# Feed-forward by pairs of batches, with the image attention of batches 2 and 3 in four half-batches inside it

## The reference

```python
x = x + _L0_xattn_ref(ctx_512, _layernorm(x), ...)       # graph attention, two layers
x = x + _L0_ffn_ref(_layernorm(x), ...)                  # 8 experts, two of them per row
x = x + _L1_xattn_ref(_layernorm(x), ctx_512, ...)       # image attention
x = x + _L1_ffn_ref(_layernorm(x), w_gate, w_up, w_down) # feed-forward, 2048 hidden columns

# image attention: p is the normalised x
kv = k_v @ W_k.T + b_k
out = einsum('bij,bjd->bid', p, kv)
sim = einsum('bid,bjd->bij', out, kv) * scale
sim = (sim - mean) * rsqrt(var + EPS) * ln_gamma + ln_beta
attn = softmax(sim)
# feed-forward: of each four hidden columns the two largest are kept
h = silu(x @ w_gate) * (x @ w_up)
out = keep_two_of_four(h) @ w_down
```

## Time and profile before

| | |
|---|---|
| median of 3 runs | 1154.78 us (1154.68 to 1155.99) |
| the profiled execution | 1155.69 us, its span 1154.0 us |
| PE busy | 976.8 us, 85% of the span |
| DVE, ACT, POOL busy | 649.3, 375.2, 264.2 us |
| bytes moved | 85.33 MB, 74 GB/s on the mean |
| mean granted TensorE clock | 0.914 |

### The profile page before, as it was taken

One profiled execution on the slowest core, in us unless ns is written; L12 is line 12 of the kernel. 1 busy time (PEld: TensorE's weight loads), 2 busy tenths in 40 slices (PEclk: granted clock), 3 DMA queues, 4 the chain that ended last, 5 costly groups with the idle time before them and its releaser, 6 DMA issues. The chain is left out here.

```text
span 1154.0 us, 15603 instructions
## 1 busy us (share of the span) xinstructions
PE 976.8 (85%) x4579; PEld 811.2 (70%) x4580; DVE 649.3 (56%) x1383; ACT 375.2 (33%) x640; POOL 264.2 (23%) x296
## 2 busy tenths in 40 slices
PE   4997459999999974333568799999999999999996
PEld 3873259999999962222456688888888888888884
DVE  7986744423443226867887445656445455664444
ACT  5875144323333323234334112222222212222120
POOL 0564033320424104467133002010030101110000
PEclk8998679999999995666679899999999999999998
DMA  8357055422634214412012001110020100000001
GB/s 315 76 139 224 10 199 172 165 99 72 204 122 145 79 40 121 149 41 69 1 37 73 1 1 37 37 35 1 0 73 0 36 0 18 18 1 1 37 37 73
DMA packets 35421, 85.33 MB, mean 74 GB/s; under 512 B 5936, under 2 KB 6064, under 8 KB 34096
## 3 DMA queue, kind: packets, MB, share of 16 engines
q1 hardware_dynamic: 26800, 61.72, 15.4%
q0 software_dynamic: 8576, 23.08, 7.6%
HBM read 61.97 MB, written 22.81 MB: 73 GB/s over the span
## 5 line engine op out<-in xcount | busy, mean ns | idle before, releaser
L72 PE MATMUL ps<-f_x_lo,f_w_hi 128*128 128x512 f32 x512 | 203.0, 396 | 13.5 <-POOL f_w_lo L1398 6.8
L73 PE MATMUL ps<-f_x_hi,f_w_lo 128*128 128x512 f32 x512 | 201.9, 394 | 0.0
L74 PE MATMUL ps<-f_x_hi,f_w_hi 128*128 128x512 f32 x512 | 201.6, 394 | 0.0
L1460 DVE TENSOR_TENSOR f_hid<-moe_rows,ps 128x512 f32<-128x512 f32 x64 | 43.7, 684 | 198.6 <-ACT moe_rows L1455 198.4
L72 PEld LDWEIGHTS ps<-f_x_lo,f_w_hi 128*128 128x128 f32 x512 | 97.7, 191 | 35.3 <-DVE f_hid L1460 7.2
L1455 ACT ACTIVATE moe_rows<-ps 128x512 f32<-128x512 f32 x64 | 38.3, 600 | 229.3 <-PE ps L74 229.1
L74 PEld LDWEIGHTS ps<-f_x_hi,f_w_hi 128*128 128x128 f32 x512 | 97.7, 191 | 20.8
L73 PEld LDWEIGHTS ps<-f_x_hi,f_w_lo 128*128 128x128 f32 x512 | 97.8, 191 | 20.4
L72 PE MATMUL ps<-gu_w_lo,m_xT_hi 128*128 (+1 forms) x312 | 106.1, 340 | 4.0 <-DVE m_xT_lo L1704 3.8
L72 PE MATMUL ps<-f_w_lo,kv_c_hi 128*128 128x512 f32 x256 | 102.3, 400 | 5.4 <-DVE x L2299 5.4
L73 PE MATMUL ps<-f_w_hi,kv_c_lo 128*128 128x512 f32 x256 | 102.2, 399 | 0.0
(11 more groups left out here) (300 smaller groups left out, 1951.3 us busy)
## 6 DMA issues: line engine op xcount, KB each, us to landing
raw<-in_moe_gu SPq DMA_DIRECT2D x32, 352.0 KB, 4.3
y_scratch<-m_y SPq DMA_DIRECT2D x39, 256.0 KB, 2.2
raw<-in_ffn_gu SPq DMA_DIRECT2D x16, 512.0 KB, 3.5
raw<-in_moe_dn SPq DMA_DIRECT2D x24, 256.0 KB
x<-in_x SPq DMA_DIRECT2D x4, 1024.0 KB, 12.0
gat_rows<-g_ybuf SPq DMA_DIRECT2D x16, 256.0 KB, 3.3
xn_scratch<-g_xn SPq DMA_DIRECT2D x16, 256.0 KB, 4.2
raw<-in_ffn_dn SPq DMA_DIRECT2D x16, 256.0 KB, 2.9
```

Of the source, the lines that this page charges most:

```text
L72: eng.matmul(out, lhs_hi, rhs_lo, start=start, stop=False)
L73: eng.matmul(out, lhs_lo, rhs_hi, start=False, stop=False)
L74: return eng.matmul(out, lhs_hi, rhs_hi, start=False, stop=stop)
L1460: dve.tensor_tensor(out, sg[:, k, :], self.UP[k], ALU.mult).then_inc(self.hid_made, 1)
```

## The change

The feed-forward takes the batches in pairs: first the four quarters of batches 0 and 1 (units 0 to 7), then those of 2 and 3 (units 8 to 15), so every weight is loaded and split twice. The image attention's block does only batches 0 and 1, and keeps the keys of batches 2 and 3. Their attention is done inside units 1 to 7 in four halves of 256 rows (h = 0 to 3). A slot is one part of one unit (slot 4n + j stands ahead of part j of unit n + 1), and a half's steps have fixed slots, counted from 6h: -1 and 0 gather the expert rows, 0 and 1 add them, 2 ACT's row sums (two passes over the row), 3 power -1/2 and normalised rows, 4 transposes, 5 `out`, 6 scores and centring, 7 scaling and exponential, 8 the sum into `X` and ACT's row sums for the feed-forward, 9 their power. The operands of batches 2 and 3 are normalised at slots 24, 25, 27, 28 and transposed at 25, 26, 28, 29. PSUM: three banks for gate and up in turn, three for the down sums, two for the attention. Silu waits for gate alone. The loops are written out. In the diff `early` holds ACT's copies (slots 6h + 4 and 6h + 5, and those of the operands), `late` its row sums (6h + 2, 6h + 8), normalised rows (6h + 3) and exponentials (6h + 7).

```diff
@@ class Units
-        self.GATE = [ps[:, 0, :], ps[:, 1, :]]
-        self.UP = [ps[:, 2, :], ps[:, 3, :]]
-        self.ACC = [ps[:, 4 + i, :] for i in range(TB)]
+        self.GU = [ps[:, k, :] for k in range(3)]
+        self.ACC = [ps[:, 3 + k, :] for k in range(3)]
...
+    def act_gate_up(self, act, s, r):
+        uses = RQ // self.SLOTS
+        act.wait_ge(self.ld_gu[r % self.SLOTS], 16 * (uses * s + r // self.SLOTS + 1))
+        if s >= 1:
+            act.wait_ge(self.products, RQ * (PAIR * s - 1) + r + 1)
+        act.copy(self.w_hi[r][:, 0:2, :], self.raw_gu[:, r % self.SLOTS, :, :]).then_inc(self.gate_up_hi, 1)
...
+    def pe_gate_up(self, pe, n, r):
...
+        for j, bank in ((0, self.gate_bank(n, r)), (1, self.up_bank(n, r))):
+            m = 2 * (RQ * n + r) + j - 3
+            if m >= 0:
+                pe.wait_ge((self.silu, self.hid_made)[m % 2], m // 2 + 1)
...
+            ins.then_inc((self.gates, self.products)[j], 1)
...
+    def pe_down(self, pe, n):
...
+        for i in range(TB):
+            if TB * n + i >= 3:
+                pe.wait_ge(self.acc_free, TB * n + i - 2)
...
@@ ffn, SyncE
+                for s in range(1, UNITS // PAIR):
+                    for r in range(2):
+                        u.load_gate_up(sp, dram["ffn_gu"], s, r)
+                    for r in range(RQ):
+                        u.load_down(sp, dram["ffn_dn"], s, r)
+                    for r in range(2, RQ):
+                        u.load_gate_up(sp, dram["ffn_gu"], s, r)
...
@@ ffn, GpSimd
+                for n in range(UNITS - 1):
+                    s, second = divmod(n + 1, PAIR)
+                    for j in range(RQ):
+                        slot_work(RQ * n + j)
+                        if second and s + 1 < UNITS // PAIR:
+                            u.pool_gate_up(pool, s + 1, j)
+                        if second and s >= 1 and j < 2:
+                            for r in (2 * j, 2 * j + 1):
+                                u.pool_down(pool, s, r)
@@ ffn, TensorE
+                for n in range(UNITS):
+                    if n + 1 < UNITS:
+                        for j in range(RQ):
+                            slot_work(RQ * n + j)
+                            if j == 0 and n + 1 in (PAIR * Q, PAIR * Q + 1):
+                                pe.wait_ge(lo_done[1], TB * (n + 2 - PAIR * Q))
+                            u.pe_gate_up(pe, n + 1, j)
+                    u.pe_down(pe, n)
@@ ffn, ScalarE
+                def row_sums(k, t, m):
...
+                    act.activation(junk[:, :], X[:, t, :], ACT.Identity,
+                                   accum_out=total[:, k, m:m + 1]).then_inc(totalled[k], 1)
+                    act.wait_ge(totalled[k], m + 1)
+                    act.activation(nmean[:, k, m:m + 1], total[:, k, m:m + 1], ACT.Identity,
+                                   scale=-1.0 / D).then_inc(meaned[k], 1)
+                    act.wait_ge(meaned[k], m + 1)
+                    act.activation(junk[:, :], X[:, t, :], ACT.Square, bias=nmean[:, k, m:m + 1],
+                                   accum_out=square[:, k, m:m + 1]).then_inc(squared[k], 1)
...
+                for n in range(1, UNITS):
+                    s, second = divmod(n, PAIR)
                     for r in range(RQ):
+                        slot = RQ * (n - 1) + r
+                        early(slot)
+                        u.act_silu(act, n, r, sg)
+                        if second and s + 1 < UNITS // PAIR:
+                            u.act_gate_up(act, s + 1, r)
+                        if second and s >= 1 and r < 2:
+                            for k in (2 * r, 2 * r + 1):
+                                u.act_down(act, s, k)
+                        late(slot)
+                    sparsify(n)
@@ ffn, VectorE
+                for n in range(1, UNITS):
+                    for r in range(RQ):
+                        slot_work(RQ * (n - 1) + r)
+                        if r == 0:
+                            dve.wait_ge(u.hid_lo_done, u.LOS * n)
+                        u.dve_hid(dve, n, r, sg, hid[:, r, :])
+                    keep_two(n, 0)
+                    evac(n - 1, (0, 1))
+                    keep_two(n, 1)
+                    for h in range(2):
+                        split(n, h)
+                    evac(n - 1, (2, 3))
+                evac(UNITS - 1, range(TB))
```

More of the change, by code:

```diff
@@ L1376, in load_down @@
[L1376 to L1388, removed]
@@ L1399, in pool_gate_up, with pool_down @@
                            self.w_hi[r][:, 0:2, :].bitcast(F32), ALU.subtract).then_inc(self.gate_up_lo, 1)
-    def pool_down(self, pool, u, r):
-        pool.wait_ge(self.down_hi, self.R * u + (r + 1))
+    def pool_down(self, pool, s, r):
+        pool.wait_ge(self.down_hi, RQ * s + r + 1)
         pool.tensor_tensor(self.w_lo[r][:, 2, :], self.raw_dn[:, r, :], self.w_hi[r][:, 2, :].bitcast(F32),
                            ALU.subtract).then_inc(self.down_lo, 1)
[L1408 to L1422, removed]
@@ L1437, in pe_rest @@
[L1437 to L1445, removed]
-            self.pe_down(pe, self.U - 1, c)
-    def act_silu(self, act, u, c, r, sg, first=False):
-        act.wait_ge(self.products, self.at(u, c, r) + 1)
-        if not (first and r < 2):
-            act.wait_ge(self.hid_made, self.at(u, c, r) - 1)
-        k = self.bank(c, r)
-        act.activation(sg[:, k, :], self.GATE[k], ACT.Silu).then_inc(self.silu, 1)
@@ new lines, in act_silu, with dve_hid @@
+    def act_silu(self, act, n, r, sg):
+        k = RQ * n + r
+        act.wait_ge(self.gates, k + 1)
+        if k >= 2:
+            act.wait_ge(self.hid_made, k - 1)
+        act.activation(sg[:, k % 2, :], self.gate_bank(n, r), ACT.Silu).then_inc(self.silu, 1)
+    def dve_hid(self, dve, n, r, sg, out):
+        k = RQ * n + r
+        dve.wait_ge(self.silu, k + 1)
+        dve.wait_ge(self.products, k + 1)
+        dve.tensor_tensor(out, sg[:, k % 2, :], self.up_bank(n, r), ALU.mult).then_inc(self.hid_made, 1)
@@ L2135, in ffn, with feed_at, four @@
+        def feed_at(m):
+            c, i = divmod(m, TB)
+            s = slice(P * i, P * i + P)
+            return u.x_hi[c][:, :, s], u.x_lo[c][:, :, s]
+        def four(bank):
+            return bank.rearrange("p (d n) -> p d n", d=DC)
         with nc.Block() as block:
@@ L2167, in _, with turn @@
             def _(pe):
-                turns = iter(range(TB, T))
-                def turn_two():
-                    for t in islice(turns, 2):
-                        norm.pe_turn(pe, t)
-                turn_two()
-                u.pe_gate_up(pe, 0, 0, tiles=range(1, RQ), first=True, between=turn_two)
-                pe.wait_ge(norm.lo_done, T)
-                u.pe_rest(pe)
+                def turn(i, k, m):
+                    pe.wait_ge(xn_ready[k], m + 1)
+                    for d in range(DC):
+                        ins = pe.transpose(AT[i][:, P * d:P * d + P], xn[:, i, P * d:P * d + P], ident[:, :])
+                    ins.then_inc(turned[k], 1)
@@ L2257, in keep_two, with add_rows @@
-                def keep_two(q, c, h):
-                    links = LINKS * 4 * q + LINKS * c + 4 * h
+                link = chain.link
+                def add_rows(h, k):
+                    for i in range(2):
+                        t = PAIR * TB + 2 * h + i
+                        dve.wait_ge(got[i], 16 * (2 * h + k + 1))
+                        if k == 1:
+                            dve.wait_ge(added, 4 * h + i + 1)
+                        dve.scalar_tensor_tensor(out=X[:, t, :], in0=xn[:, i, :], scalar=rt["weight"][:, t, k:k + 1],
+                                                 in1=X[:, t, :], op0=ALU.mult, op1=ALU.add).then_inc(added, 1)
```

687 lines of the change are left out of this document (409 added, 278 removed).

## The result

The changed kernel is slower: median 1174.87 us (1173.97 to 1176.61, four runs) against 1154.73 (1154.26 to 1155.99) in the same session, ratio 1.0167 with an interval of 1.0155 to 1.0180 (the two medians alone give 1.0174, which lies inside it). Its profiled span is 1172.4 us against 1154.0, +18.4; the mean granted clock 0.911.

A forecast was written before the change was run, and what follows sets the result against it. PE bounds the feed-forward units; it is mostly idle in the attention ahead. Terms -57.3 - 6.3 + 18.7 + 43.8 + 11.5 + 6.7 sum to +17.1, 1172 us in the runs, taken as 1170 for overlapping waits; range 1138 to 1190.

The forecast's parts named there:

- The block's start: Feed-forward block's start: two batches of attention leave the front, so it starts at 536 instead of 593.3, -57.3 us (-52 to -61).
- The 27.5 us of DVE's work for batch 1: Before PE's first part: 18 us of batch 1's own work plus 9.5 for statistics, normalising, two transposes' wait and `lo`.
- The first unit: Start of the block to unit 1's gate and up end: 4 tiles turned, not 12, -6.3 us (-3 to -8).
- PE's added work: Attention inside the units: four half-batches of 3.9 us, plus 3.2 for turning 8 tiles, +18.7 us (17 to 22).
- PE's waits in units 1 to 8: PE waiting for down banks, row sums and normalised rows in in-order queues: +43.8 us (19 to 65).
- rival 1: Waits in the units close up because DVE and ACT have room: faster, 1139 us; chance 0.22.
- The clock: Matmuls at the lower clock behind the five waits over 4 us: +11.5 us (0 to 30).
- Units 9 to 15: Fourth down tile waits 2.2 us in units 9, 11, 13, late third load adding nothing beyond: +6.7 us (0 to 10).
- Rival 2: Whole kernel breaks even, with stalls of 45 us in all: 1155 us; chance 0.07.
- Rival 4: On ACT, a Silu/exponential table switch holds it twice the row's 1.28 us, eight times: 1177 us; chance 0.05.
- Rival 3: PE's clock does not recover: units 3 to 8 have ten waits, 2.8 us each, delays handed on: 1194 us; chance 0.10.
- Rival 5: Less than two batches leaves the front; if the feed-forward block starts at 545, 1179 us; chance 0.06.

The follow-up runs named there:

- the best version: Changed kernel plus four edits: first down bank freed earlier, weight loads asked for earlier, row sums two slots later, unit 7's rows ahead of weight copies: 1142.55 us, ratio 0.9882.

## Why the prediction was right, and where its terms were off

The forecast was 1170 us and slower; it came at 1174.87. The direction and the mechanism were right: the front gains two batches of attention, and the in-order queues, the third down bank and the lower clock behind the waits take more than that back. The closeness is in part luck. The sum was +17.1 and the span gave +18.4, but under it the terms were off by up to 8 us in both directions: the start by +4.0, the waits of units 1 to 8 by -8.4, the clock there by +3.0, the units behind by +5.2. Two of the signs that would have shown it wrong were near: under 30 us of waits (35.4 came), and a block that ends after 540 (it ended at 540.0).

*The block's start*: -53.3 instead of -57.3, in the bounds. The step "Batch 0 runs as it did, less POOL's adds beside it: it ends near 501" failed: batch 1's first centring starts at 502.97, before at 502.46. From batch 0's first centring (471.51, before 470.51) that is 31.5 us instead of 32.0, so POOL's adds had held up half a microsecond at most; the other 1.0 was lost ahead of that, and differs between executions: without the attention in the units, with the same front, PE's first part comes 1.2 us earlier (530.03). The 27.5 us of DVE's work for batch 1 held well: PE's first part comes at 531.23, 28.3 later. In it lie 2.88 us of DVE waiting for the third tile's scores, and one scaling of 2.90 us instead of 0.74 beside POOL's first subtraction; the 7.4 for the part itself came as 8.3. The chain (DVE twice, POOL, PE):

```profile
513.35 0.74 DVE L1994 SCALAR_TENSOR_TENSOR kv_c_raw<-kv_c_raw,a_rs,k_beta 128x512 f32<-128x512 f32 x1
...
521.14 2.90 DVE L1994 SCALAR_TENSOR_TENSOR kv_c_raw<-kv_c_raw,a_rs,k_beta 128x512 f32<-128x512 f32 x1
...
521.16 2.33 POOL L1394 TENSOR_TENSOR f_w_lo<-raw,f_w_hi 128x1024 fp32r<-128x1024 f32 x1
...
531.23 0.79 PE L73 MATMUL ps<-f_x_lo,f_w_hi 128*128 128x512 f32 x1 [1.93 <-DVE f_x_lo L169]
```

*The first unit*: -6.8, as predicted (-6.3), with the wait for Silu that was named (5.77 us, to 580.15, 40.2 us behind the block's start; 40.6 predicted).

*PE's added work*: about 17.6 instead of 18.7; twelve matmuls of 256 columns take 1.43 us, 0.119 each, where 0.14 was taken between two sizes.

*PE's waits in units 1 to 8*: 35.4 instead of 43.8; this term was the worst sized. The places were right, nearly every size too large: slot 10 7.39 for 9.6 (its own times, 20.8 less 10.9, give 9.9), slot 26 5.86 for 6.3, slot 25 3.04 for 3.4, slot 22 1.67 for 2.6, unit 7's bank 1.04 for 2.9, unit 4's 2.35 for 5.6. The longest single wait was unit 5's for a bank, not slot 10's as said, though the four in front of transposes still add to more (18.0) than the six for a bank (13.8). Even units without attention had none, as said. A row sum was taken as 1.9 us, and takes 1.84:

```profile
655.75 0.63 ACT L2264 ACTIVATE raw<-x 128x512 bf16<-128x512 f32 x1
...
656.74 0.72 ACT L2270 ACTIVATE raw<-x,f_nmean 128x512 bf16<-128x512 f32 x1
...
663.09 0.58 ACT L1435 ACTIVATE moe_rows<-ps 128x512 f32<-128x512 f32 x1
```

Four tiles hold ACT from 655.75 to the next Silu at 663.09, 7.3 us (7.5 predicted): rival 1's condition, "if a row sum costs under 1 us", is refuted. What made the sum too large is, most likely, that each wait was counted from the undelayed schedule; PE's earlier pauses gave ACT and DVE time for the next. The run that frees the first bank earlier shows this from the other side: with 17.8 us of bank waits gone, the waits for rows, `lo` and products grew by 9.4.

One place was too small: unit 5's bank, 7.79 for 4.3. The prediction had the power behind the subtraction whose weights land late, and that is there. It had neither the gather that DVE waits for in the same slot nor the collision behind both. DVE, then POOL and ACT:

```profile
763.60 1.82 DVE L2362 SCALAR_TENSOR_TENSOR x<-moe_rows,weight,x 128x512 f32<-128x512 f32 x2 [5.49 <-DMA moe_rows<-y_scratch,slot]
765.38 2.90 DVE L2381 SCALAR_TENSOR_TENSOR kv_c_raw<-kv_c_raw,kv_wk_raw,k_beta 128x512 f32<-128x512 f32 x1
...
770.29 0.68 DVE L1441 TENSOR_TENSOR f_hid<-moe_rows,ps 128x512 f32<-128x512 f32 x1
...
761.81 2.40 POOL L1394 TENSOR_TENSOR f_w_lo<-raw,f_w_hi 128x1024 fp32r<-128x1024 f32 x1 [2.21 <-ACT f_w_hi L1384]
764.16 1.18 POOL L2182 TENSOR_TENSOR kv_wk_raw<-kv_wk_raw,minus_half 128x2 f32<-128x2 f32 x1
765.33 2.39 POOL L1394 TENSOR_TENSOR f_w_lo<-raw,f_w_hi 128x1024 fp32r<-128x1024 f32 x1
...
760.68 1.05 ACT L1384 CAST f_w_hi<-raw 128x1024 fp32r<-128x1024 f32 x1 [6.31 <-DMA raw<-in_ffn_gu]
```

The gathered rows are added by 765.42 and the power is there at 765.34: two waits end together, so ending one of them earlier should not help by itself. Then the scaling meets the next subtraction. The unit's last product (770.29) comes 8.6 us after its gate and up matmuls end at 761.73. With the loads moved this pause falls to 5.61, in the best version to 2.60. The gather stands in POOL's queue too, so all three hang on POOL's subtractions: with the narrow ones, on top of the moved loads, the gathered rows' addition starts 2.9 us ahead of the end of the gate and up matmuls (757.29 to 760.22; here 1.9 behind it), the scaling takes 0.75, and the pause falls from 5.61 to 2.44. What each of the three is worth alone was not tried.

*The clock*: of the 67.5 us in these units 35.4 are waits and 17.6 work; the other 14.5 are matmuls at the lower clock, 11.5 predicted. About 11.4 of them show in the feed-forward's own matmuls (242.6 us without the waits, 231.1 before), the rest in transposes behind waits. That term hid part of the error in the waits.

*Units 9 to 15*: +11.9 for +6.7. The failing step is "it costs nothing but its share of the 2.2", said of the third part's load. That the load comes late was right (ACT waits for `raw<-in_ffn_gu` 29.5 us in seven waits), its price was not: moving the loads gave 10.8 us over the whole kernel, 8.5 of them here, so that these units cost 3.4 us more than before with the loads moved, and 11.9 without. The late copy also holds the Silu and the absolute values behind it, and so starts the comparisons a microsecond later, which the step left out. The three pauses are 2.49, 2.59 and 3.18 where 2.2 each was said (8.3 for 6.7), and the matmuls around them add 3.7 at the lower clock, for which the step had nothing. So units 9, 11 and 13 took 37.3, 35.8 and 38.0 us where 33 to 35 was named as a sign.

*The rivals.* Rival 2 (1155) is refuted by the time. Rival 1's amounts of added work were near for DVE (56 us for its 54) and not for ACT (72 for its 100). Rival 4 is refuted: the table load behind slot 7's exponentials takes its 1.28 us, with Silu right behind. The two ACT rows:

```profile
651.92 1.28 ACT L1435 ACT_TABLE_LOAD   x1
653.22 0.60 ACT L1435 ACTIVATE moe_rows<-ps 128x512 f32<-128x512 f32 x1
```

The Trainium skill (ScalarE: Activation LUTs, What ACT_TABLE_LOAD costs) counts a drain on top, about 2.66 us in all; here 1.30 us lie from one start to the next. Rival 3's slow clock came to 14.5 us in these units, near the forecast's 11.5 and not its own 27.5 and more. Rival 5 came half way, 540.0 for its 545 and the forecast's 536. Rival 1's time, 1139, came out after all, but for the four edits (1142.55), not for the change as written.

## What to carry to other kernels

Work moved into the shadow of a busy engine is paid by its place in the other engines' queues, not by their busy share: DVE was busy for 61% and ACT for 42% of the seven units that lost 67 us. Follow every queue that an order touches before changing it: the same steps with four small moves (row sums two slots later, loads asked for earlier, the first bank freed earlier, unit 7's rows first) turned 1.7% slower into 1.2% faster. And when banks are taken from a rotation, time the slack of the one that comes due first, with the slowest instance of the instructions ahead of it: here it was worked out as 0.2 us, and ACT's row sums (unit 4), its late copies and POOL's subtractions (units 9, 11 and 13) each used it up.

## What the runs showed of the hardware that was not expected

**Two engines and one port.** A two-input DVE instruction of 0.74 us takes 2.90 when it starts beside POOL's subtraction of 2.33 us (521.14 and 521.16 above), and three comparisons take 3.23 to 4.10 instead of 1.90. POOL's own duration (2.33 to 2.40) is near the 2.41 of the earlier trace rows; but the pair of subtractions beside the longest comparisons (998.81) takes 5.57, where those of units 9 and 13 take 4.76 and 4.78, so POOL can lose time too. With the subtractions cut to 8 columns, beside the moved loads, DVE was back at 1.90, and the kernel 9.9 us faster. The Trainium skill (SBUF — State Buffer, Who interferes with whom) has DVE instructions with two SBUF inputs exclude a GpSimd one that reads SBUF, the whole instruction long. The rows agree in the main: DVE's instruction ends 0.55 us behind POOL's here (524.04 to 523.49), and 0.56 behind it in unit 5 (768.28 to 767.72), so all but 0.2 of its own 0.74 lie behind POOL's.

**The clock behind short pauses.** Behind unit 9's wait of 2.49 us PE starts at the full pace of 0.23 us, and drops to 0.43, at the lower of its two levels (1.2 GHz), a microsecond later:

```profile
939.47 0.39 PE L75 MATMUL ps<-f_w_hi,kv_c_hi 128*128 128x512 f32 x1
939.70 0.48 PE L73 MATMUL ps<-f_w_lo,kv_c_hi 128*128 128x512 f32 x1
939.97 0.63 PE L74 MATMUL ps<-f_w_hi,kv_c_lo 128*128 128x512 f32 x1
940.40 0.63 PE L75 MATMUL ps<-f_w_hi,kv_c_hi 128*128 128x512 f32 x1
```

It stays there until 943.34. The product takes 15.49 us, 1.8 more than 11.20 + 2.49. Unit 11's takes 14.04 with a wait of 2.59, 0.3 more; with the 0.95 us wait of the moved loads unit 9's is 12.41, 0.3 more. The prediction put a price only on pauses over 4 us; pauses of 2.5 us paid it in some cases and not in others, and what decides is left open.
